# Two output projections, a gate computation and a cast chain moved to later steps of a round schedule

## The reference, cut to what matters

```python
h = h.transpose(0, 2, 1, 3).reshape(Bsz, Nn, C)
gates = jax.nn.softmax(h @ Wr.T + br, axis=-1)
_, idx = jax.lax.top_k(gates, ROUTED_HEADS)
mask = jax.nn.one_hot(idx, H - SHARED_HEADS, dtype=gates.dtype).sum(axis=-2)
routed_gates = gates * mask * ROUTED_HEADS
sw = jax.nn.softmax(h @ Ws.T + bs, axis=-1)
shared_gates = sw * SHARED_HEADS
weight_0 = sw * 2.0
shared_gates = weight_0[..., 0:1] * shared_gates
routed_gates = weight_0[..., 1:2] * routed_gates
masked_gates = jnp.concatenate([shared_gates, routed_gates], axis=-1)
out = h * masked_gates.sum(axis=-1, keepdims=True)
return out @ Wp.T + bp
```

## Time and profile before

| what | value |
|---|---|
| median of 3 executions | 4480.93 us (4480.48 to 4482.56) |
| the profiled execution's own time | 4479.25 us |
| its span, first to last instruction | 4477.1 us |
| mean granted TensorE clock | 0.982 |
| PE busy | 4224.6 us (94%) |
| DVE busy | 2965.5 us (66%) |
| ACT busy | 2542.5 us (57%) |
| POOL busy | 811.8 us (18%) |

### The profile page before, as it was taken

The page is one execution under the profiler, slowest core; times in us unless marked ns, Lnnn a source line. Parts: engine busy times, 40 slices in busy tenths (PEclk is TensorE's granted clock), DMA queues, the critical chain, the costliest instruction groups (busy, mean ns, idle before and its releaser), DMA issues. The chain is left out here.

```text
span 4477.1 us, 66439 instructions
## 1 busy us (share of the span) xinstructions
PE 4224.6 (94%) x23716; PEld 2400.0 (54%) x23750; DVE 2965.5 (66%) x7431; ACT 2542.5 (57%) x6408; POOL 811.8 (18%) x576
## 2 busy tenths in 40 slices
PE   6999999999999997888989999999999998999999
PEld 2343344444343342577446666666666665556555
DVE  5767777777777675967765677676676766334333
ACT  3767666666666765743546676767777675111111
POOL 2322444443322311622000000000000000000000
PEclk9999999999999998999999999999999999999999
DMA  8456455445455461000100100110101102000000
GB/s 160 74 78 85 65 66 80 60 64 68 68 75 83 66 83 61 1 20 10 76 12 27 37 30 28 32 32 27 32 27 32 33 26 73 5 5 5 10 5 10
DMA packets 182844, 204.97 MB, mean 46 GB/s; under 512 B 44651, under 2 KB 165099, under 8 KB 180854
## 3 DMA queue, kind: packets, MB, share of 16 engines
q1 hardware_dynamic: 180886, 199.15, 24.3%
q10 hardware_dynamic: 1632, 1.57, 0.3%
HBM read 139.90 MB, written 60.78 MB: 45 GB/s over the span
## 5 line engine op out<-in xcount | busy, mean ns | idle before, releaser
L485 DVE TENSOR_REDUCE L0x_maxes<-L0x_ps_max 128x1 f32<-128x512 f32 x1536 | 976.2, 683 | 288.6 <-PE L0x_ps_max L760 287.0
L671 ACT ACTIVATE L0x_probs<-L0x_ps_sc 128x512 f32<-128x512 f32 x1536 | 822.6, 607 | 360.7 <-PE L0x_ps_sc L750 356.7
L760 PE MATMUL L0x_ps_max<-L0x_kstack,L0x_qstack 96*128 96x512 bf16 x1536 | 587.3, 383 | 22.6 <-DVE L0x_maxes L485 21.3
L2765 ACT ACTIVATE L3x_pexp<-L3x_ps,L3x_nmax 128x77 f32<-128x77 f32 (+2 forms) x1536 | 601.4, 433 | 0.0
L750 PE MATMUL L0x_ps_sc<-L0x_qstack,L0x_kstack 104*128 104x512 bf16 x1536 | 557.0, 383 | 11.5 <-ACT L0x_probs L671 11.0
L2647 DVE TENSOR_REDUCE L3x_nmax<-L3x_ps 128x2 f32<-128x154 f32 (+2 forms) x768 | 346.3, 506 | 242.5 <-PE L3x_ps L2878 240.1
L2773 ACT COPY L3x_pT<-L3x_ps 128x512 f32<-128x512 f32 x512 | 275.1, 593 | 225.8 <-PE L3x_ps L2886 225.4
L2265 ACT ACTIVATE L3f_act_g<-L3f_ps_gu 128x512 f32<-128x512 f32 x128 | 76.4, 597 | 542.4 <-PE L3f_ps_gu L2311 542.3
L774 PE MATMUL L0x_ps_out<-L0x_probs,L0x_vpad 128*32 128x512 f32 x3072 | 369.4, 598 | 1.1 <-ACT L0x_probs L671 1.1
L2663 DVE TENSOR_SCALAR L3x_pexp<-L3x_pexp,L3x_rsum 128x77 f32<-128x77 f32 (+2 forms) x1536 | 357.7, 305 | 6.8
L2765 ACT ACTIVATION_READ_ACCUMULATOR L3x_pexp<-L3x_ps,L3x_nmax 128x1 f32 x1536 | 359.6, 235 | 0.0
(11 more groups left out here) (377 smaller groups left out, 6823.5 us busy)
## 6 DMA issues: line engine op xcount, KB each, us to landing
L0x_kstack<-parts_scratch SPq DMA_DIRECT2D x141, 256.0 KB, 10.0
L0x_qstack<-parts_scratch SPq DMA_DIRECT2D x141, 256.0 KB, 14.5
parts_scratch<-L0x_kparts SPq DMA_DIRECT2D x24, 768.0 KB, 3.7
parts_scratch<-L0x_qparts SPq DMA_DIRECT2D x24, 768.0 KB, 5.0
rel_scratch<-L3x_rel_e SPq DMA_DIRECT2D x32, 408.0 KB, 2.4
L3x_rel_d<-prob_scratch SPq DMA_DIRECT2D x32, 408.0 KB, 3.1
L0x_kv_in<-in_ctxT SPq DMA_DIRECT2D x16, 512.0 KB, 4.2
L3x_rel_t<-rel_scratch SPq DMA_DIRECT2D x32, 154.0 KB, 2.3
```

The source lines that it names most:

```text
L485: V.tensor_reduce(maxes[:, t, head:head + 1], ps_max[:, q.count(64, unit) % BANKS, :], AX.X, ALU.max).then_inc(max_taken, 1)
L671: nc.scalar.activation(probs[:, step % SLOTS, j], ps_sc[:, at % BANKS, :], ACT.Exp, scale=HD ** -0.5).then_inc(probs_ready, 1)
L760: nc.tensor.matmul(ps_max[:, at % BANKS, :], qstack[q.parity][0:ROWS, head, t * P:(t + 1) * P], kstack[q.parity][0:ROWS, head, :], start=T ...
L2765: i = nc.scalar.activation(pexp[:, n % 4, e, a:b], ps[:, SB + 2 * (n % 2) + e, a:b], ACT.Exp, bias=nmax[:, n % 4, s, e:e + 1], accum_out=s ...
```

## The change

In the table the mixture's y0 moves from step 22 to step 24, and y1 from step 24 to step 26, behind raw1 of step 25. `gate_scale` moves from step 21 to step 23. On POOL the two halves of the q split of a mixture item move from steps 22 and 23 to steps 25 and 26; those of a cross item stay. The additions of y to x on POOL follow y to steps 24 and 26. No instruction is added, removed or changed in shape.

```diff
--- before.py
+++ after.py
@@ -125,7 +125,7 @@
     "mixture": [(2, "v", 0), (3, "v", 1), (4, "raw", 3), (5, "negmax", 1), (7, "xnT", 0), (8, "xnT", 1),
                 (9, "q", 0), (10, "q", 1), (11, "hT", 0), (12, "hT", 1), (13, "negmax", 2), (14, "k", 0),
                 (15, "raw", 0), (16, "k", 1), (18, "gates", 0), (19, "qT", 0), (20, "qT", 1), (21, "negmax", 3),
-                (22, "y", 0), (24, "y", 1), (25, "raw", 1), (29, "negmax", 0), (31, "raw", 2)],
+                (24, "y", 0), (25, "raw", 1), (26, "y", 1), (29, "negmax", 0), (31, "raw", 2)],
 }
 
 FIRST = [(2, "k", 0), (3, "k", 1), (14, "xnT", 0), (18, "xnT", 1), (24, "q", 0), (26, "q", 1), (29, "v", 0),
@@ -422,9 +422,10 @@
                         pool.wait_ge(negmax_ready, q.plus(1).count(4, 1))
                     if ahead.later and after_k in (0, 1):
                         split(ahead, taken["k"], ahead.count(2, 2), kf, kparts, k_step, k_split, after_k)
-                    if ahead.later and after_q in (1, 2):
+                    split_at = 1 if ahead.cross else 4
+                    if ahead.later and after_q in (split_at, split_at + 1):
                         here, there = (taken["q"], ahead.count(2, 2)) if ahead.cross else (taken["qT"], ahead.own(2, 2))
-                        split(ahead, here, there, qf, qparts, q_step, q_split, after_q - 1)
+                        split(ahead, here, there, qf, qparts, q_step, q_split, after_q - split_at)
 
             nc.gpsimd.memset(vpad[0][:], 1.0).then_inc(vpad_ones, 1)
             nc.gpsimd.memset(vpad[1][:], 1.0).then_inc(vpad_ones, 1)
@@ -624,7 +625,7 @@
                             negated(own, (m % STEPS) // 8)
                     if prev.there and not prev.cross and n == 20:
                         gates_after_exp(prev)
-                    if prev.there and not prev.cross and n == 21:
+                    if prev.there and not prev.cross and n == 23:
                         gate_scale(prev)
                     if q.number == -1 and n == 16:
```

## The result

The changed kernel takes 4489.61 us (median of 15 executions; 4484.29 to 4496.38), beside 4480.48 us (4476.19 to 4483.08) for the kernel before on the same chip. The ratio is 1.0023, 95% interval 1.0015 to 1.003: some 9 us more, where 4491 was forecast. The profiled execution took 4494.78 us, so it lies 5.2 us above the median.

The account below looks back on a forecast made before the run. No engine is full; handing over between PE, DVE and ACT through three banks and one turn bank bounds a round. 4479.25 - 3.6 (rounds 9 to 13) + 13.5 (14 to 16) = 4489.15 us profiled, median 4491; range 4481 to 4499.

Parts of the forecast that it names:

- The holding by POOL, and where it goes in rounds 9 to 13: Rounds 9 to 13: gate_scale held once, not three times; the q split meets step 27's negation; 1.6 us gained a round.
- The clock in rounds 9 to 13: Rounds 9 to 13: the 1.7 us pause brings the clock down in three rounds of five, at 1.6 us each.
- likeliest case: Whole kernel: as forecast, slower by 5 to 15 us, 4486 to 4496 us; chance 0.50.
- Rival E: More clock falls, before the negmax turn or twice in the long pause: +8 us over rounds 9 to 13, 4499; chance 0.10.
- Rounds 14 to 16: Rounds 14 to 16: gate_scale held and y1 ahead of q1 cost 8.4 us, clock falls 5.1; 13.5 us lost in all.
- each long pause brings a fall: Rounds 14 to 16: PE's 3.1 us pause before q0 brings a clock fall in each, 1.7 us apiece.
- The sum: Whole kernel: 4479.25 - 3.6 + 13.5 = 4489.15 us for a profiled execution; median 1.68 above, given as 4491.
- Rival C: Rounds 9 to 13: gate arithmetic escapes POOL, 4.4 us less each, 4468 to 4472 us in all; chance 0.09.
- What costs nothing: The later q split of mixture items and y's additions, 2 to 4 us later, are covered; rounds 0 to 8 and 17 on keep their order.

Follow-up runs that it names:

- e8: The changed kernel with the q split of rounds 9 to 13 moved behind the negation of step 27: 4488.82 us, ratio 1.002.
- e3: The change made for mixture items 8 to 12 alone (rounds 9 to 13), items 13 to 15 as in the kernel before: 4484.53 us, ratio 1.0002.
- e5: The changed kernel with the k split's second half in rounds 14 to 16 queued behind y0's addition again: 4489.06 us, ratio 1.0018.
- e2: The changed kernel with the q split put back at steps 22 and 23: 4506.43 us, ratio 1.0058.
- e9: The change for items 13 to 15 alone (rounds 14 to 16), every mixture q split where the kernel before had it: 4491.08 us, ratio 1.0024.
- e6: The kernel before with, in rounds 9 to 13, the k split's second half behind y0's addition and the q split behind y1's: 4464.81 us, ratio 0.9963.
- e7: e6 with the q split of rounds 9 to 13 also moved behind the negation of step 27: 4461.39 us, ratio 0.9957.
- e1: The changed kernel with gate_scale back at step 21 and the q split at 22 and 23, only y0 and y1 moved: 4522.67 us, ratio 1.0094.
- e11: The kernel before with both halves of the k split queued ahead of y0's addition in rounds 14 to 16: 4496.78 us, ratio 1.0033.

## Why the prediction was right, and where its terms were off

**The holding by POOL, and where it goes in rounds 9 to 13: right.** The first gate operation was forecast at 1.5 us and took 1.47, the third and fifth at 0.16; the pause before raw1 at 1.7, and was 1.73; line 493 at 0.8 to 1.3, and took 0.80. A round without a fall takes 74.10, where the average was 75.62: 1.5 gained, against 1.6 forecast. But this gain is the fall of the clock that stays away, not shorter waits: PE's two pauses add up to 3.04 us where one of 2.55 was, and a round of 75.32 before, less the 1.65 that a fall costs (e8), would be 73.67, an estimate, or 0.4 us under the 74.10. So all of the gain hung on the clock. That line 493 is held, as the earlier trace rows had it, is borne out: it takes 0.80 us beside the split and 0.18 without it. The Trainium skill's sentence on one SBUF input (SBUF — State Buffer, section "Who interferes with whom") holds outside the two-port modes only, and the same section lists tensor_scalar among the operations that can enter one; whether that is the reason, no run here shows.

**The clock in rounds 9 to 13: the term that was mis-sized.** The forecast took three falls of five behind the 1.7 us pause and left the 1.31 us one out of its likeliest case, as it is near the 1.19 us that never brought one. The runs show both to be enough. The changed kernel had four falls, one behind the first pause and three behind the second, one of them 6.8 us long: 7.8 us in all where 4.8 was counted. So the term is 5 x (-1.52) + 7.8 = +0.2 in place of -3.6. That was no odd execution: in e3 and e5, with the same rounds 9 to 13, the clock fell in all ten rounds, and they took 379.9 and 381.5 us. Rival E had the place, at twice the price.

**Rounds 14 to 16: right in the waits, open in the falls.** The hold was put on the third gate operation; in rounds 14 and 15 it was the second (line 573), as the first began 0.1 us before POOL's operation ended and got through, and in round 16 the first (1.71 us). The end is the same. The waits cost 3.2 and 2.3 us in rounds 15 and 16 without a fall, and falls another 77.57 - 74.92 = 2.7 and 76.15 - 74.70 = 1.5; with round 14 (77.35 - 72.58 = 4.8) the sum is 14.3, against 13.5 forecast. That each long pause brings a fall is only half right: in rounds 15 and 16 of the changed kernel's profile (pauses of 3.26 and 2.72 us) falls stood with it, in round 14 the fall was in step 18, behind the turn of the gates, and none came behind the pause of 3.25 us; and in e2, e8 and e9 the same pauses in rounds 15 and 16 came without one. Where they stay away the loss is 10.2 to 11.7 us, 2 to 3 less than was forecast.

**The sum.** Against the profiled execution the forecast of 4489.15 was 5.6 us low: 3.8 from rounds 9 to 13, 0.8 from 14 to 16, 2.6 from round 0, which no step covers, and the rest of the kernel gave 1.6 back. The median lies 5.2 below that execution, which is why 4491 came so near. No profile shows the median's own rounds; a likely reason is that fewer falls come in rounds 14 to 16, and then two misses offset each other, some 4 us or more too little for rounds 9 to 13 and 2 to 3 too much for 14 to 16. The mechanism and the side are the forecast's merit; that it came within 1.4 us is luck. Rival C (the gates escape POOL) did not occur, yet e6 and e7 put it at 3.6 to 4.0 us a round, near the 4.4 given: in these runs it was POOL's work that had to be moved, not DVE's.

**What costs nothing: right, as far as seen.** Rounds 6 to 8 and 17 keep their times to 0.01 us with the q split three steps later.

Open is why the clock falls behind one pause and not behind an equal one in the next round. The rounds without a fall show only that it isn't the length of the pause alone.

## What to carry to other kernels

Before a chain of tiny operations is moved, look at what runs on POOL beside it: here moving DVE's chain by two steps and PE's turns with it changed which operation was held and gained nothing, while a parting of the k split's two halves around an addition that POOL has to wait for anyway, with the q split moved behind it, gave 0.4%. If two pieces of POOL work are kept apart by a third, moving that third joins them: read the order of the queue after the edit, as y0's addition left in rounds 14 to 16 what it had split. And a shorter wait may be worth less than its difference: pauses of 1.7 and 1.3 us brought the clock down in four rounds of five (in e3 and e5 in all ten), where one of 2.55 us did in five, at 1.6 us a fall. Read the clock of more than one profiled execution before a part of the time is put down to it.

## What the runs showed of the hardware that was not expected

- A fall of the clock to 0.5 (the 1.2 GHz level) lasted 3.4 us, in some rounds 6.8 or (e1, e11) 10.2, and cost 75.13 - 73.48 = 1.65 us for 3.4 us and 77.18 - 74.10 = 3.1 for 6.8. It came behind pauses of 1.31 us (three of the changed kernel's rounds), of 1.73 us (four of five rounds in e8, one of five in the changed kernel) and behind 16 matmuls of 17 columns with a pause of 0.32 us (rounds 14 to 16 of e5, but in none of these rounds before). It did not come behind pauses of 3.26 us in round 15 of e9 and of 3.25 us in round 14 of the changed kernel.
- A DVE operation of 4 elements a partition (0.16 us) took 1.74 to 2.13 us beside a POOL operation of 128x1024, always until that one's end. Held were those with two SBUF inputs and the TENSOR_SCALAR from f32 to bf16 (0.18 to 0.80 and 1.26 us). Not held were the reductions, operations that were issued in the 0.08 us between two POOL operations, and one that was issued 0.1 us before a POOL operation ended (line 571 in round 15 of the changed kernel, 0.16 us).
